# A fused token encoder, attention and routed LSTM kernel: cell work one unit later, fronts begun six units early, values' transfers from Sync, a feature-major projection

## The chip, the cores and the metric

The kernel runs on one core of one Trainium2 chip. The metric is the device time of one execution in microseconds (us): the median of three runs of the kernel before is 1920.38 us (1920.33 to 1920.73). The five engines are called PE (TensorE), DVE (VectorE), ACT (ScalarE), POOL (GpSimd) and SP (Sync, which here only issues transfers). Each runs its own list of instructions in order, and they meet at semaphores alone.

## What is computed

Sixteen sequences of 512 tokens go through three layers. The reference, cut to what matters:

```python
h = tok(x)                                    # embedding (89) next to an upsampled |STFT| projection (39)
h = h + attn(layernorm(h))                    # 8 heads of 16; 64 summary tokens and 448 feature tokens
h = h + ffn(layernorm(h))                     # top-2 of 8 LSTM experts

def attn(x):
    Q, K, V = split(x @ W_qkv + b_qkv)        # Q scaled
    out_wtok = softmax(Qw . Kcat) . Vcat      # each summary token over its own 7 feature tokens and itself
    w_wtok = softmax(Qf . out_wtok) per chunk # one weight of a feature token for its summary
    w_fea = softmax(Qf . K window of 17)      # local window
    out_fea = w_wtok * out_wtok + w_fea . V window
    return out @ W_out + b_out

def expert(x_seq, Wi, Wh, b, Wo, bo):         # scan over the 16 sequences, all 512 tokens side by side
    gates = xt @ Wi + h @ Wh + b
    c = sigmoid(f) * c + sigmoid(i) * tanh(g)
    h = sigmoid(o) * tanh(c)
    return h @ Wo + bo
# logits -> top 2 -> softmax of two; expert inputs are masked; y = sum of mask * weight * expert output
```

The scan is over the 16 sequences, so the LSTM state of 8 experts times 2 choices times 512 tokens passes from one sequence to the next.

## The kernel before

**Steps and units.** A step is one sequence. A step of the LSTM part has 32 units, `t = 0..31`, four for each expert `e = t // 4`: gates I, G, F, O in this order, `g = t % 4`. A unit on PE (`unit_gate`, L506) is twelve matmuls of 128x128 weights and 512 columns: input and state, each as three half-precision products for two choices. The timeline prints them as x6 from `xm` and x6 from `Hs`. Its result lies in one of two PSUM slots. ACT takes it out with a tanh (`gate_tanh`, L655), which frees the slot for the unit after next. DVE makes the cell and the hidden state: `input_part` (L1007), `cell` (L1013, L1017), `hidden` (L992), `hidden_lo` (L997), `chosen` (L1028, L1032, the tokens' choice times its weight), and `masked_input` (L985), which writes `xm`, the masked input of an expert that PE reads from the expert's unit I on. ACT adds `cell_tanh` (L662) and `split_hi` (L666, the upper half of the hidden state), on which `hidden_lo` waits. `unit_y` (L512) is the output matmul of an expert.

**Fronts.** Everything that a sequence needs before its LSTM step (embedding, layer norm, attention, second norm, logits, choice, masks) is its front: some 45 pieces, which `front(t, b)` of each engine issues in unit `t` of the step before. Which piece goes to which unit is set by the tables `SP_AT`, `PE_AT`, `ACT_AT` and `DVE_AT` (from L56). So every engine's list is written out by hand: step work and front pieces take turns, and each piece waits for the other engines by a semaphore of its own. Pieces of the front that are named below: `xn` (L795, layer norm's output), `p_lo` (L878) and `p_T` (L882, transposed window weights), `values` (L459, 84 small matmuls of window weights by values), `window` (L447, 84 of queries by keys), `proj` (L465, L466, attention's projection and its bias), `logits` (L477), `maskT` (L483), `emb` (L420). Queries and values go to a block-diagonal tile `diag` by four transfers each, from SP (queries, L284) and from ACT's own queue (values, L619), because the diagonal blocks lie on other partitions' columns.

**Masks.** At the end of a front the masks go to DRAM and come back spread over 128 partitions (`mask_in`, L338), and `masked_input` of the next step's expert 0 reads them in unit 30 (`XM_AT`).

The first front has no LSTM step to hide it and takes until 118.8 us; step 0 has no state term and no F gate; steps 1 to 14 are alike; step 15 has no front.

## Time and profile before

| | |
|---|---|
| median of three runs | 1920.38 us |
| the profiled execution | 1918.11 us, its span 1916.3 us |
| PE busy | 1729.1 us, 90% of the span |
| DVE busy | 1559.5 us, 81% |
| ACT busy | 991.9 us, 52% |
| POOL busy | 65.2 us, 3% |
| gate matmuls (L506) | 5904, 1451.6 us busy |
| chain that ended last | PE 40%, DVE 33%, DMA 8%, issue 7%, ACT 5%, ACT's queue 4% |
| mean granted clock of PE | 0.97 of full speed |

Busy time of an engine is a share of the span. The timeline prints instructions in order of time, merged where alike; the last bracket is the time that the engine sat idle before the row, and who ended it. A matmul's own duration has its way through the array in it, so the distance from one start to the next is what it costs PE.

### The profile page before, as it was taken

What the parts mean: (1) busy time and instruction counts of PE and PEld (TensorE: products, weight loads), DVE (VectorE), ACT (ScalarE), POOL (GpSimd) and SP (SyncE); (2) the same over time, 40 slices, a digit from 0 to 9 for tenths busy, and PEclk for the clock granted to TensorE, in tenths of its full rate; (3) what the DMA queues carried; (4) which work ended last, traced back from release to release, by engine and by line L of the source; (5) the groups of instructions that cost most, each with busy time, mean ns of one, the idle gap of its engine ahead of it and who ended that gap; (6) DMA issues with size and microseconds to landing.
All of it is one profiled execution on the core that took longest, in us unless ns stands there. A gap on an engine that the chain in (4) does not pass through costs nothing.

```text
span 1916.3 us, 25885 instructions
## 1 busy us (share of the span) xinstructions
PE 1729.1 (90%) x9898; PEld 837.6 (44%) x9898; DVE 1559.5 (81%) x2433; ACT 991.9 (52%) x1114; POOL 65.2 (3%) x42
## 2 busy tenths in 40 slices
PE   3457799999999999999999999999999999999998
PEld 2223344444444444444444444444444444444443
DVE  2649698897988889798898988889898888979865
ACT  3234554646555555645545455455555555564544
POOL 1000000000000000000000000000000000000000
PEclk9668899999999999999999999999999999999999
DMA  3113241413314132232313224151331413223221
GB/s 114 20 41 74 57 67 46 77 37 67 63 49 74 39 70 52 52 70 51 67 45 69 51 57 67 44 80 37 63 66 46 76 37 71 53 50 67 55 61 36
DMA packets 318594, 110.95 MB, mean 58 GB/s; under 512 B 240331, under 2 KB 299581, under 8 KB 318471
## 3 DMA queue, kind: packets, MB, share of 16 engines
q1 hardware_dynamic: 202758, 101.96, 23.9%
q10 hardware_dynamic: 115712, 7.34, 3.8%
q8 instruction: 78, 1.28, 0.3%
q14 instruction: 46, 0.37, 0.1%
HBM read 89.84 MB, written 4.74 MB: 49 GB/s over the span
## 4 chain that ended last, share of the span: by engine, by line
PE 40%; DVE 33%; DMA 8%; issue 7%; ACT 5%; ACTq 4%; SPq 1%; POOL 0%; DVEq 0%
PE gates L506 25%; ACTq L619 4%; DVE C L1017 4%; DVE tmp L1007 4%; DMA masks<-mask_scratch 3%; DVE tmp L1013 3%; DMA prod<-in_x_ids 3%; DVE xm L985 3%; PE yp L512 3%; DVE Hs L997 3%; DVE tmp L1028 3%; DVE xn L795 2%; PE FA L447 2%; ACT tmp L655 2%; PE FA L459 2%
## 5 line engine op out<-in xcount | busy, mean ns | idle before, releaser
L655 ACT ACTIVATE tmp<-gates,bias_sb 128x1024 f32<-128x1024 f32 x504 | 557.5, 1109 | 558.6 <-PE gates L506 496.1
L506 PE MATMUL gates<-xm,wi_sb 128*128 128x512 f16 x3024 | 747.3, 384 | 46.2 <-ACT tmp L655 31.0
L506 PE MATMUL gates<-Hs,wh_sb 128*128 128x512 f16 x2880 | 704.4, 381 | 0.0
L506 PEld LDWEIGHTS gates<-xm,wi_sb 128*128 128x128 f16 x3024 | 290.3, 99 | 435.3 <-issue 105.1
L506 PEld LDWEIGHTS gates<-Hs,wh_sb 128*128 128x128 f16 x2880 | 283.2, 98 | 344.3 <-issue 8.0
L662 ACT ACTIVATE tmp<-C 128x1024 f32<-128x1024 f32 x128 | 135.2, 1057 | 226.4 <-DVE C L1017 223.2
L992 DVE SCALAR_TENSOR_TENSOR tmp<-tmp 128x1024 f32<-128x1024 f32 x128 | 155.9, 1218 | 71.8 <-ACT tmp L662 71.8
L1007 DVE SCALAR_TENSOR_TENSOR tmp<-tmp 128x1024 f32<-128x1024 f32 x120 | 144.9, 1208 | 46.4 <-ACT tmp L655 44.9
L985 DVE TENSOR_TENSOR xm<-xs,masks 128x2048 f16<-128x2048 f16 x128 | 155.2, 1212 | 32.7 <-DMA masks<-mask_scratch 32.7
L997 DVE SCALAR_TENSOR_TENSOR Hs<-tmp,Hs 128x1024 f16<-128x1024 f32 x120 | 146.4, 1220 | 37.7 <-ACT Hs L666 36.7
L1013 DVE SCALAR_TENSOR_TENSOR tmp<-tmp,C 128x1024 f32<-128x1024 f32 x120 | 146.4, 1220 | 14.4 <-ACT tmp L655 14.0
L1017 DVE SCALAR_TENSOR_TENSOR C<-tmp 128x1024 f32<-128x1024 f32 x120 | 147.0, 1225 | 4.1
L666 ACT ACTIVATE Hs<-tmp 128x1024 f16<-128x1024 f32 x120 | 126.5, 1055 | 31.2 <-DVE tmp L992 30.7
L512 PE MATMUL yp<-z,wo_sb 128*128 128x512 f32 x256 | 134.9, 609 | 8.2 <-DVE z L1032 8.2
L1105 POOL TENSOR_TENSOR rstd<-veps,mhalf 128x4 f32<-128x4 f32 x32 | 61.6, 1926 | 1682.6 <-DVE veps L922 1114.8
L1032 DVE TENSOR_TENSOR z<-tmp,roww 128x512 f32<-128x512 f32 x128 | 88.6, 692 | 13.6 <-DVE tmp L1028 0.5
L1028 DVE COPY_PREDICATED tmp<-rowk,tmp 128x512 f32<-128x512 uint16 x128 | 93.0, 727 | 0.1
L512 PEld LDWEIGHTS yp<-z,wo_sb 128*128 128x128 f32 x256 | 48.0, 194 | 38.8 <-issue 12.2
L459 PE MATMUL FA<-vwin,diag 128*128 128x32 f16 x1344 | 36.3, 177 | 7.4 <-DVE vwin L882 7.4
L447 PEld LDWEIGHTS FA<-xn,diag 128*128 128x128 f16 x1344 | 38.2, 97 | 8.1 <-issue 5.5
L459 PEld LDWEIGHTS FA<-vwin,diag 128*128 128x128 f16 x1344 | 36.0, 96 | 12.5 <-DVE vwin L882 9.2
L447 PE MATMUL FA<-xn,diag 128*128 128x32 f16 x1344 | 39.1, 178 | 0.0
(155 smaller groups left out, 1218.9 us busy)
## 6 DMA issues: line engine op xcount, KB each, us to landing
masks<-mask_scratch SPq DMA_DIRECT2D x128, 256.0 KB, 5.0
roww<-mw_scratch SPq DMA_DIRECT2D x128, 256.0 KB, 4.0
rowk<-mask_scratch SPq DMA_DIRECT2D x128, 128.0 KB, 3.0
diag<-pr SPq DMA_DIRECT2D x64, 112.0 KB, 4.3
diag<-vwin ACTq DMA_DIRECT2D x64, 112.0 KB, 4.8
out_dram<-h SPq DMA_DIRECT2D x16, 256.0 KB, 3.7
C<-in_wi SPq DMA_DIRECT2D x1, 2048.0 KB, 10.9
C<-in_wh SPq DMA_DIRECT2D x1, 2048.0 KB, 15.6
```

The costliest lines, as they stand in the source:

```text
L506: last = mm(gates[:, slot, k * SEQ:(k + 1) * SEQ], w, v, start=(i < K), stop=(i >= len(seq) - K))
L512: mm(yp[:, :], wo_sb[:, e, :], z32[:, :], start=False, stop=(e == E - 1)).then_inc(s_y, 1)
L655: A(tmp[:, gate_at(gate, e), :], gates[:, (n - 1) % 2, :], ACT.Tanh, bias=bias_sb[:, e, gate:gate + 1], scale=UNSCALE).then_inc(s_tanh, 1)
L662: A(tmp[:, TANH_C, :], C[:, e, :], ACT.Tanh, scale=0.5).then_inc(s_tc, 1)
L666: A(Hs[:, e, HI, :], tmp[:, gate_at(O, e), :], ACT.Copy, scale=V_SCALE).then_inc(s_hhi, 1)
L985: TT(xm[:, e % 2, :, :, :], xv, mv_, ALU.mult).then_inc(s_xm, 1)
L992: STT(out=at, in0=at, scalar=1.0, in1=tmp[:, TANH_C, :], op0=ALU.add, op1=ALU.mult).then_inc(s_h, 1)
L997: STT(out=Hs[:, e, LO, :], in0=tmp[:, gate_at(O, e), :], scalar=V_SCALE, in1=Hs[:, e, HI, :], op0=ALU.mult, op1=ALU.subtract).then_inc(s_h ...
L1007: STT(out=at_i, in0=at_i, scalar=1.0, in1=at_g, op0=ALU.add, op1=ALU.mult).then_inc(s_u, 1)
L1013: STT(out=at_f, in0=at_f, scalar=1.0, in1=C[:, e, :], op0=ALU.add, op1=ALU.mult).then_inc(s_v, 1)
L1017: STT(out=C[:, e, :], in0=at_f, scalar=0.5, in1=tmp[:, gate_at(I, e), :], op0=ALU.mult, op1=ALU.add).then_inc(s_c, 1)
L1028: V.copy_predicated(at[:, 0:SEQ], rowk1[:, e % 2, :].bitcast(u16), at[:, SEQ:2 * SEQ]).then_inc(s_sel, 1)
```

## The change

It has these parts:

1. **Cell work a unit later.** `cell(e)` moves from unit 4e+2 to 4e+4, `cell_tanh` from 4e+3 to 4e+4, `hidden` from 4e+4 to 4e+5, `input_part` from 4e+1 to 4e+2, `split_hi` from 4e+4 to 4e+6, `hidden_lo` from 4e+5 to 4e+7, `chosen` from 4e+6 to 4e+7, `unit_y` from unit 4e+8 to 4e+9. The F gate (and tanh of the cell in it) has two buffers in place of one, and `z32` is gone.
2. **Fronts six units early.** `run_front` lets a front begin at unit -6, that is unit 26 of the step before; nearly all pieces move 2 to 4 units earlier.
3. **Values** are interleaved (upper and lower half next to each other, 4 bytes), transposed once as 4-byte words, and sent to `diag` by four transfers from SP in unit 7. `diag` is interleaved too, so the weights of `window` and `values` are read with a step of two elements.
4. **The projection** is one 128x512 matmul, feature-major, a copy with the bias on ACT, and four transposes back.
5. `masked_input` for the next step's expert 0 moves from the start of unit 30 to the end of unit 31; the weights' rows go out by a transfer and a semaphore of their own (`wout`).

```diff
-    SP_AT = dict(ids=0, qbd=6, rows=28)
-    PE_AT = dict(emb=1, xT=3, qkv=4, summary=7, window=8, feature=14, values=18, proj=21, x2T=23,
+    SP_AT = dict(ids=-6, qbd=3, vz=7, rows=27, wrow=30)
+    PE_AT = dict(emb=-3, xT=0, qkv=1, summary=4, window=6, feature=12, values=16, proj=18, projT=19, x2T=23,
                  logits=24, maskT=27)
-    DVE_AT = dict(onehot=0, moments=1, xn=2, pw=5, q_lo=5, kv_lo=6, v_win=7, w_max=8, s_max=9, s_sub=10, w_sum=11,
-                  w_out=12, s_sum=13, s_norm=14, f_max=15, p_lo=16, p_T=16, f_sum=17, f_part=18, attn=19,
-                  moments2=21, xn2=22, x_lo=24, choice1=25, choice2=25, weights=26)
-    MASKS_AT = 29
+    DVE_AT = dict(onehot=-4, moments=-2, xn=-1, pw=2, q_lo=2, kv_lo=3, v_win=4, w_max=5, s_max=7, s_sub=8, w_sum=9,
+                  w_out=10, s_sum=11, s_norm=12, f_max=13, p_lo=14, p_T=15, f_sum=16, f_part=16, attn=17,
+                  moments2=20, xn2=21, x_lo=24, choice1=24, choice2=25, weights=26)
+    EARLY = 6
+    MASKS_AT = 28
-    XM_AT = 30
+    XM_AT = 31
...
+        def run_front(front, t, s):
+            if s == 0 and t == 0:
+                for u in range(-EARLY, 0):
+                    front(u, 1)
+            if s + 1 < STEPS:
+                front(t, s + 1)
+            if s + 2 < STEPS and t >= NG * E - EARLY:
+                front(t - NG * E, s + 2)
...
+                if t == SP_AT["vz"]:
+                    sp.wait_ge(S["vwin"], b + 1)
+                    sp.wait_ge(S["S"], b + 1)
+                    for g in range(NG):
+                        load(diag[32 * g:32 * g + 32, :, g, :], vwj[32 * g:32 * g + 32, :, :], S["vz"])
...
                 if t == PE_AT["proj"]:
                     pe.wait_ge(S["attn"], b1)
+                    mm(FA[:, 1, :], wout_sb[:, :], attn[:, :], start=True, stop=True).then_inc(S["projT"], 1)
+                if t == PE_AT["projT"]:
+                    pe.wait_ge(S["projS"], b1)
                     for i in range(TILES):
-                        mm(FB[:, i * D:(i + 1) * D], attn[:, i * P:(i + 1) * P], wout_sb[:, :], start=True, stop=False)
-                        last = mm(FB[:, i * D:(i + 1) * D], ones1[:, :], bout_sb[:, :], start=False, stop=True)
+                        last = nc.tensor.transpose(FB[:, i * D:(i + 1) * D], xnT[:, i * P:(i + 1) * P], ident[:, :])
...
-                    for v in (HI, LO):
-                        own = vhl[:, v, :]
-                        win = bass.AP(tensor=own.tensor, offset=own.offset, ap=[list(own.ap[0]), [QB, NBLK], [1, KB]])
-                        last = V.transpose(vw16[:, v, :, :], win)
-                    last.then_inc(S["vwin"], 1)
+                    win = bass.AP(tensor=vp.tensor, offset=vp.offset, ap=[list(vp.ap[0]), [QB, NBLK], [1, KB]])
+                    V.transpose(vwj, win).then_inc(S["vwin"], 1)
...
+                    if g == 0 and e and not first:
+                        cell(s, e - 1)
+                    elif g == 0 and s >= 2 and not e:
+                        cell(s - 1, E - 1)
                     if g == 1 and e < E - 1:
                         masked_input(s, e + 1, par, first and e == 0)
-                    if g == 1 and e and not last:
+                    if g == 3 and e and not last:
                         hidden_lo(s, e - 1)
...
-                    if t == XM_AT and not last:
-                        masked_input(s + 1, 0, 1 - par, False)
-                    if g == 2 and e:
+                    if g == 3 and e:
                         chosen(s, e - 1)
...
+                    run_front(lambda u, b: front(u, b, b % 2), t, s)
+                    if g == 1 and e:
+                        hidden(s, e - 1)
...
+                    if g == 2:
                         input_part(s, e, first)
-                    if g == 2 and not first:
-                        cell(s, e)
+                    if t == XM_AT and not last:
+                        masked_input(s + 1, 0, 1 - par, False)
```

**How the rows move: the end of a step on DVE.** These are DVE's rows of the kernel before from `hidden_lo` of expert 6 (written `Hs`) to the first `cell` (`C`) of the last expert; the `xm` row is the masked input on which unit 0 of the next step waits. The bracket is what a row waits for.

```order
L997 SCALAR_TENSOR_TENSOR Hs<-tmp,Hs 128x1024 [waits s_hhi]
L1007 SCALAR_TENSOR_TENSOR tmp<-tmp 128x1024 [waits s_tanh]
L985 TENSOR_TENSOR xm<-xs,masks 128x2048 [waits s_gate,f_xlo,s_mask_in0]
L1028 COPY_PREDICATED tmp<-rowk,tmp 128x512 [waits s_hlo,s_row_in0]
L1032 TENSOR_TENSOR z<-tmp,roww 128x512 [waits s_sel,s_y]
L1013 SCALAR_TENSOR_TENSOR tmp<-tmp,C 128x1024 [waits s_tanh]
L1017 SCALAR_TENSOR_TENSOR C<-tmp 128x1024 [waits s_u,s_v]
```

And these are the same rows of the changed kernel, from `input_part` of expert 7 (L1028 there) on:

```order
L1028 SCALAR_TENSOR_TENSOR tmp<-tmp 128x1024 [waits s_tanh]
L1018 SCALAR_TENSOR_TENSOR Hs<-tmp,Hs 128x1024 [waits s_hhi]
L1049 COPY_PREDICATED tmp<-rowk,tmp 128x512 [waits s_hlo,s_row_in0]
L1051 TENSOR_TENSOR tmp<-tmp,roww 128x512 [waits s_sel]
L819 TENSOR_SCALAR xn<-h_sb,mv,rstd 128x128 [waits f_rstd]
L819 TENSOR_SCALAR xn<-h_sb,mv,rstd 128x128 x3
L1006 TENSOR_TENSOR xm<-xs,masks 128x2048 [waits s_gate,f_xlo,s_mask_in0]
```

What moved: `xm` stood behind `hidden_lo` by one row of unit 29 and ahead of `chosen`; now it stands behind `hidden_lo`, `chosen` and the four rows of the next front's `xn`, and `hidden_lo` itself stands in unit 31.

**The same place on ACT**, in the changed kernel: the tanh rows (L678) are those of units 28, 29, 30 and 31, and L689 is `split_hi` of expert 6, which releases the `Hs` row above (`s_hhi`).

```order
L678 ACTIVATE tmp<-gates,bias_sb 128x1024 [waits s_c,s_gate]
L685 ACTIVATE tmp<-C 128x1024 [waits s_c]
L678 ACTIVATE tmp<-gates,bias_sb 128x1024 [waits s_c,s_gate]
L605 ACTIVATE h_sb<-FB 128x512 [waits f_h2,f_emb]
L678 ACTIVATE tmp<-gates,bias_sb 128x1024 [waits s_h,s_gate]
L689 ACTIVATE Hs<-tmp 128x1024 [waits s_h]
L678 ACTIVATE tmp<-gates,bias_sb 128x1024 [waits s_y,s_gate]
```

What moved: `split_hi` came in unit 28 behind one tanh; it now comes behind the tanh of unit 30.

**The window weights on DVE.** Before, `p_T` (L882) follows `p_lo` (L878) at once, in unit 16, and PE's `values` wait for it after unit 18:

```order
L992 SCALAR_TENSOR_TENSOR tmp<-tmp 128x1024 [waits s_tanh,s_tc]
L878 SCALAR_TENSOR_TENSOR pr<-vwin,pr 128x896 [waits f_phi]
L882 STREAM_TRANSPOSE vwin<-pr 128x896 [waits f_plo]
L985 TENSOR_TENSOR xm<-xs,masks 128x2048 [waits s_gate,s_mask_in1]
L997 SCALAR_TENSOR_TENSOR Hs<-tmp,Hs 128x1024 [waits s_hhi]
```

Now, in units 13 to 15, with PE's `values` after unit 16:

```order
L1013 SCALAR_TENSOR_TENSOR tmp<-tmp 128x1024 [waits s_tanh,s_tc]
L899 SCALAR_TENSOR_TENSOR pr<-vwin,pr 128x896 [waits f_phi]
L1028 SCALAR_TENSOR_TENSOR tmp<-tmp 128x1024 [waits s_tanh]
L1018 SCALAR_TENSOR_TENSOR Hs<-tmp,Hs 128x1024 [waits s_hhi]
L1049 COPY_PREDICATED tmp<-rowk,tmp 128x512 [waits s_hlo,s_row_in0]
L1051 TENSOR_TENSOR tmp<-tmp,roww 128x512 [waits s_sel]
L903 STREAM_TRANSPOSE vwin<-pr 128x896 [waits f_plo]
```

What moved: `p_T` stands behind `input_part`, `hidden_lo` and `chosen`, in the unit right ahead of the one after which PE wants it, instead of two units ahead.

## Rows read from the trace of the kernel before

**Rows 1.** Busy time and PE's timeline, one step from its unit 18 to the next
```profile
core 0: us, PE busy (x) PEld busy (x) DVE busy (x) ACT busy (x) POOL busy (x), PEclk, DMA share, GB/s
624.55:738.61 114.06, 108.16 (x631) 52.45 (x631) 98.08 (x153) 61.72 (x70) 3.82 (x2) 1.00 0.28 58
...
624.55 1.47 PE L506 MATMUL gates<-xm,wi_sb 128*128 128x512 f16 x6 [1.46 <-ACT tmp L655]
...
661.03 0.63 PE L483 MATMUL FB<-ident,pr 128*72 128x128 f32 x4 [1.15 <-DVE pr L973]
```

**Rows 2.** Timeline of ACT behind its four transfers of values
```profile
717.80 2.12 ACT L655 ACTIVATE tmp<-gates,bias_sb 128x1024 f32<-128x1024 f32 x2 [3.09 <-issue]
```

**Rows 3.** Timeline of PE: projection, one output matmul, logits
```profile
637.88 0.38 PE L465 MATMUL FB<-wout_sb,attn 128*128 128x128 f32 x2
...
641.10 1.47 PE L506 MATMUL gates<-xm,wi_sb 128*128 128x512 f16 x6
...
650.15 1.02 PE L512 MATMUL yp<-z,wo_sb 128*128 128x512 f32 x2
651.04 1.06 PE L477 MATMUL FA<-rw_sb,xnT 128*128 128x8 f32 x8
651.95 1.46 PE L506 MATMUL gates<-xm,wi_sb 128*128 128x512 f16 x6
```

**Rows 4.** Timeline of all engines around the end of a step
```profile
666.58 1.05 ACT L666 ACTIVATE Hs<-tmp 128x1024 f16<-128x1024 f32 x1
667.53 1.46 PE L506 MATMUL gates<-xm,wi_sb 128*128 128x512 f16 x6
667.66 1.23 DVE L997 SCALAR_TENSOR_TENSOR Hs<-tmp,Hs 128x1024 f16<-128x1024 f32 x1 [1.94 <-ACT Hs L666]
667.74 1.11 ACT L655 ACTIVATE tmp<-gates,bias_sb 128x1024 f32<-128x1024 f32 x1
...
671.49 1.23 DVE L985 TENSOR_TENSOR xm<-xs,masks 128x2048 f16<-128x2048 f16 x1 [1.38 <-DMA masks<-mask_scratch]
...
672.82 1.46 PE L506 MATMUL gates<-xm,wi_sb 128*128 128x512 f16 x6
```

**Rows 5.** Timeline of DVE: durations of pieces, and a stretch without idle time
```profile
624.86 1.11 DVE L882 STREAM_TRANSPOSE vwin<-pr 128x896 f32<-128x896 f32 x1
...
630.32 0.72 DVE L1028 COPY_PREDICATED tmp<-rowk,tmp 128x512 f32<-128x512 uint16 x1
...
631.76 0.22 DVE L892 TENSOR_TENSOR red<-oW,red 128x64 f32<-128x64 f32 x1
...
645.90 1.11 DVE L795 TENSOR_SCALAR xn<-h,mv,rstd 128x128 f32<-128x128 f32 x4
...
725.80 1.22 DVE L985 TENSOR_TENSOR xm<-xs,masks 128x2048 f16<-128x2048 f16 x1
...
737.68 1.18 DVE L878 SCALAR_TENSOR_TENSOR pr<-vwin,pr 128x896 f16<-128x896 f32 x1
```

**Rows 6.** Timeline of PE: the 84 matmuls of `values`
```profile
627.15 2.25 PE L459 MATMUL FA<-vwin,diag 128*128 128x32 f16 x84
629.25 1.46 PE L506 MATMUL gates<-xm,wi_sb 128*128 128x512 f16 x6
```

**Rows 7.** PE's timeline in step 0, and two short stretches with the clock (columns as in rows 1)
```profile
207.19 1.07 PE L483 MATMUL FB<-ident,pr 128*72 128x128 f32 x4 [5.46 <-DVE pr L973]
...
216.71 1.83 PE L506 MATMUL gates<-xm,wi_sb 128*128 128x512 f16 x6 [2.37 <-issue]
...
207.20:210.70 3.50, 3.50 (x11) 1.89 (x12) 1.07 (x1) 1.17 (x2) 0.00 (x0) 0.50 0.61 120
217.50:220.90 3.40, 3.40 (x11) 1.35 (x9) 1.69 (x2) 0.00 (x0) 0.00 (x0) 0.52 0.20 58
```

**Rows 8.** Transfers by issue: count, size, us from issue to landing
```profile
diag<-pr SPq DMA_DIRECT2D x64, 112.0 KB, 4.3
diag<-vwin ACTq DMA_DIRECT2D x64, 112.0 KB, 4.8
```

More of the change, by code:

```diff
@@ L361, in step @@
                     e, g = t // NG, t % NG
-                    if t == 9 and not first:
+                    if t == 10 and not first:
                         store(s - 1, 1 - par)
-                    if not last:
-                        front(t, s + 1)
+                    run_front(front, t, s)
                     if g == 1 and e < E - 2:
@@ L373, in step @@
                         rows_in(s + 1, 0)
-            for t in range(NG * E):
+            for t in range(-EARLY, NG * E):
                 front(t, 0)
@@ L532, in step @@
                         unit_gate(s, e, g, first)
-                    if g == 0 and e == 2:
+                    if g == 1 and e == 2:
                         y_bias(s)
-                    if g == 0 and e >= 2:
+                    if g == 1 and e >= 2:
                         unit_y(s, e - 2)
-                    elif g == 0 and not first:
+                    elif g == 1 and not first:
                         unit_y(s - 1, e - 2 + E)
@@ L540, in step @@
                         y_back(s - 1)
-                    if not last:
-                        front(t, s + 1)
+                    run_front(front, t, s)
             pe.wait_ge(s_const, 16 * len(consts))
             pe.wait_ge(s_zero, 1)
-            pe.wait_ge(s_prep, 4)
-            for t in range(NG * E):
+            pe.wait_ge(s_prep, 3)
+            for t in range(-EARLY, NG * E):
                 front(t, 0)
@@ L659, in cell_tanh @@
                 act.wait_ge(s_c, s * E + e + 1)
-                if s == 0 and e:
-                    act.wait_ge(s_h, e)
-                A(tmp[:, TANH_C, :], C[:, e, :], ACT.Tanh, scale=0.5).then_inc(s_tc, 1)
+                if s == 0 and e >= 2:
+                    act.wait_ge(s_h, e - 1)
+                A(tmp[:, gate_at(F, e), :], C[:, e, :], ACT.Tanh, scale=0.5).then_inc(s_tc, 1)
             def split_hi(s, e):
@@ L678, in step @@
                         y_out(s - 1)
-                    if g == 0 and e and not last:
+                    if g == 0 and e:
+                        cell_tanh(s, e - 1)
+                    elif g == 0 and not first:
+                        cell_tanh(s - 1, E - 1)
+                    if g == 2 and e and not last:
                         split_hi(s, e - 1)
-                    elif g == 0 and not e and not first:
+                    elif g == 2 and not e and not first:
                         split_hi(s - 1, E - 1)
-                    if g == 3:
-                        cell_tanh(s, e)
-                    if not last:
-                        front(t, s + 1)
+                    run_front(front, t, s)
             par_of = lambda b: PAR[0]
@@ L706, in _ @@
             split_w_hi(wh_st, wh_sb, 0.5, s_wh_load)
-            for t in range(NG * E):
+            for t in range(-EARLY, NG * E):
                 front(t, 0)
@@ L714, in _ @@
             run_steps(step_p)
+            cell_tanh(STEPS - 1, E - 1)
             y_out(STEPS - 1)
@@ L1061, in step @@
                         add_y(s - 1, 1 - par)
-                    if not last:
-                        front(t, s + 1, 1 - par)
-                    if g == 1:
+                    run_front(lambda u, b: front(u, b, b % 2), t, s)
+                    if g == 1 and e:
+                        hidden(s, e - 1)
+                    elif g == 1 and not first:
+                        hidden(s - 1, E - 1)
+                    if g == 2:
                         input_part(s, e, first)
-                    if g == 2 and not first:
-                        cell(s, e)
+                    if t == XM_AT and not last:
+                        masked_input(s + 1, 0, 1 - par, False)
             dve.wait_ge(s_zero, 1)
-            for t in range(NG * E):
+            for t in range(-EARLY, NG * E):
                 front(t, 0, 0)
@@ L1081, in _ @@
             run_steps(step)
+            cell(STEPS - 1, E - 1)
             hidden(STEPS - 1, E - 1)
@@ L1107, in step @@
             def step(s, par, first, last):
-                if not last:
-                    for t in range(NG * E):
-                        front(t, s + 1)
+                for t in range(NG * E):
+                    run_front(front, t, s)
             pool.wait_ge(s_zero, 1)
-            for t in range(NG * E):
+            for t in range(-EARLY, NG * E):
                 front(t, 0)
```

108 lines of the change are left out of this document (53 added, 55 removed).

## The prediction

> **What bounds the kernel now.** The page comes first: PE is busy for 90% of the span, DVE for 81%, and steps 1 to 14 look alike, so I read one step closely. From unit 18 of one step to unit 18 of the next there are 114.06 us, of which PE is busy for 108.16, DVE for 98.1 and ACT for 61.7 [rows 1]. The reader is to see three things. PE does the most, and idles for 5.9 us a step. That idle time is a few waits of about 1 us for ACT or DVE, two of which are shown [rows 1]. And DVE, with 86% of the step, has little room where the front is dense. The average step is 114.0 us: unit 0 of step 1 starts at 216.71 [rows 7], unit 0 of step 5 at 672.82 [rows 4], a fourth of the difference. The sum therefore is: PE's own work per step, plus the waits that remain or appear, against 114.0, times 14.
>
> The timelines of ACT and DVE then tell where waits come from. The longest idle time on ACT that is nobody's work is 3.09 us behind its own four transfers of values [rows 2]: a tanh is late, DVE waits for it, and PE for the next one.
>
> **PE's own work.** The projection costs PE 641.10 - 637.88 = 3.22 us [rows 3]. The new one is one 128x512 matmul in full precision, like the output matmul, 651.04 - 650.15 = 0.89 us, and four transposes, 0.63 at most as `maskT` shows [rows 1]: 1.5 us. That takes off 1.7 and leaves 108.2 - 1.7 = 106.5 us per step. The new copy on ACT (0.6 to 0.7) lies beside unit 19. The strided weights of `window` and `values` I cost at nothing, see below.
>
> **The waits that go.** ACT no longer issues the values' transfers, which takes the 3.1 us out of unit 9 and 10. SP does it in unit 7; behind it on SP stand rows for `chosen` eight units later, so its wait for the window scores delays nobody. DVE transposes once instead of twice, 1.1 us less. `emb`, `xT` and `x2T` get one more unit between DVE's piece and PE's, and the token ids are fetched in unit 26 for a piece in unit 28. If I walk PE and DVE through the step with durations of the trace, all 5.9 us of old waits go: what I find late in their place is next.
>
> **A new wait at the end of a step.** PE's unit 0 reads `xm`. In the kernel before, `xm` came in unit 30, waited for the masks' transfer, and was just in time: it ended at 672.72 and PE began at 672.82 [rows 4]. Now it is the last of a chain that can't start before PE ends unit 30. Tanh starts 0.21 after the unit's matmuls are through (a tanh at 667.74 behind a unit that ended at 667.53) and lasts 1.11; `split_hi` to `hidden_lo` is 667.66 - 666.58 = 1.08; `hidden_lo` lasts 1.23 [rows 4]; `chosen` takes 631.76 - 630.32 = 1.44, the four pieces of `xn` 1.11 [rows 5]; `xm` 1.23 and 0.10 to PE [rows 4]. The sum is 7.5 us. In the meantime PE has only unit 31, which is half of 672.72 - 667.53, 2.6 us. So PE waits 4.9 us, in every step, whatever DVE did before. Moving `xm` to unit 31 costs nothing only where DVE runs ahead of PE, and here the chain forbids it.
>
> **A new wait before `values`.** DVE's `hidden_lo` of unit 11 can't start before unit 10 ends plus 0.21 + 1.11 + 1.08 = 2.4 us. From there to `p_lo` DVE has the same nine pieces as in the stretch from 725.80 to 737.68, which had no idle time: `xm`, `hidden_lo`, `s_sum`, `input_part`, `chosen`, `s_norm`, `cell`, `f_max`, `hidden`, 11.9 us; `p_lo` adds 1.18 [rows 5]. Then follow `hidden_lo` 1.23, `chosen` 1.44 and `p_T` 1.11: 2.4 + 11.9 + 1.2 + 3.8 = 19.3 us after unit 10. PE arrives there after six units (15.6), one output matmul (0.9) and the matmul of the feature scores (0.8): 17.3. It waits 2.0 us. Before, `p_T` stood two units ahead of `values` and this wait did not exist.
>
> With both, a step has 106.5 + 4.9 + 2.0 = 113.4 us, 0.6 less than now. The work saved is about given back.
>
> **The clock.** What decides is what such gaps do to PE's clock. In step 0, PE idles 5.46 us before 207.19, and in the next 3.5 us its granted clock is 0.50, the lower level of 1.2 GHz; it idles 2.37 before 216.71, and the next 3.4 us are at 0.52 [rows 7]. In the step of rows 1, with waits of 1.5 at most, it stays at 1.00. At half speed and fully busy, 3.4 us lose 1.7. After 4.9 us of idle time I count that loss in every step. After 2.0 us, which is less than the 2.37 shown and more than the 1.5 shown, I take half of it, 0.9. So a step has 113.4 + 1.7 + 0.9 = 116.0 us, 2.0 more than now, and 14 steps have 28 us more. The bounds are no loss (113.4) and both in full (116.8).
>
> **What runs once.** In the first front the chain goes through both sets of transfers, 4.3 and 4.8 us to landing [rows 8], with pieces twice as long now; through the projection, at the slow clock; and through one transpose fewer: between 0 and some 8 us less. In step 0 six units of the next front stand in unit 0, where PE must wait for each, up to 6 us more; the last boundary lacks `xn`, 1 us less. I take -4 together, between -9 and +5.
>
> **Strided weights.** The 84 matmuls of `values` take 2.10 us, 25 ns each with their weights, which lie packed [rows 6]. No row shows weights with a step of two. The nearest row for slow weight loads are the eight full-precision ones of `logits`, 0.91 us, 114 ns each [rows 3]. So the price lies between 0 and 84 x 89 ns = 7.5 us for each of two groups per step. I take 0, since the moving operand of `values` has that step already. The Trainium skill's page "TensorE: Matmul & The Clock Gate", section "Weight-path perf modes — Fast Weight Load (FWL) and DoubleRow", says that half-precision weights load fast, packed or strided, for column steps up to 1,024 elements; by it the price is 0. No run here shows it yet, and by the other end the sum would be 240 us higher.
>
> **Sum.** 1918.11 (this execution) + 28 - 4 = 1942; the median of the runs is 2.3 above this execution, so 1944 us.
>
> **The rivals.**
> - *The clock holds.* The gaps are there but each falls so that the clock stays up, or falls only while PE idles. For it: in steps 1 to 14 the clock is near 1 although there are waits. Against: both gaps of rows 7. Then 14 x -0.6 - 4 = -12: 1908 us. This is the case on the other side. It decides at a loss of 0.6 us per step: with less, the kernel is faster.
> - *The waits are hidden* because DVE's and ACT's new slack is larger than I read it, and PE runs without waits. 14 x (106.5 - 114.0) - 4 = -109: 1811 us. Against it: the order of ACT and DVE makes both chains hard.
> - *Strided weights load slowly.* Two groups per step; with a third of the bound, 2.5 us each, 16 x 5 = 80 more: about 2020, at the bound 2180.
> - *The parts cancel*, for instance if the clock falls at the boundary alone and the loss overlaps the gap by half (0.85): 14 x 0.2 - 4, about 1919.
>
> **Chances.** A measurement of this kernel can tell some 0.2% from no change, 4 us. The forecast (both waits and the clock) gets 0.62, the strided weights 0.08: slower 0.70. The clock holding gets 0.14 and the hidden waits 0.06: faster 0.20. Cancelling gets 0.10, and is the chance of no difference. The range goes from just under the clock holding, 1907, to both losses in full and the upper bound of what runs once, 1920.4 + 14 x 2.8 + 5 = 1965, taken as 1966; it leaves out the hidden waits, the slow weights and a small tail, under 0.2.
>
> **What would show it.** PE idles for about 4.9 us before unit 0 of each step, and the waits put it down to `xm`; it idles for about 2 before the first matmul of `values`, put down to `p_T`; the granted clock reads 0.5 for a stretch behind unit 0 of nearly all steps, and the mean is below 0.97. The waits behind ACT's issue are gone, and the projection costs 1.5 us. If a step is 113.4 with the clock at 1.00, the clock was wrong; if PE does not wait at unit 0, the chain was; if `values` takes more than 2.1 us between its neighbours, the weights were.

## The result: 0.3% slower, and where the expected 1% went

The changed kernel takes 1926.62 us (median of 8 runs, 1923.51 to 1927.87) against 1920.36 for the kernel before (8 runs, 1917.91 to 1922.06) in the same session: ratio 1.0032, 95% interval 1.0021 to 1.0043. That is 6.3 us slower where 24 were forecast. The time lies in the range; the change was forecast almost four times too large.

| | before | after |
|---|---|---|
| span of the profiled execution | 1916.3 us | 1924.2 us |
| PE busy | 1729.1 us | 1720.4 us |
| DVE busy | 1559.5 us | 1548.0 us |
| mean granted clock | 0.97 | 0.946 |
| start of unit 0 in step 1 (us from the span's start) | 216.71 | 208.97 |
| start of unit 0 in step 15 | 1812.41 | 1817.50 |

The last two rows split the result. Ahead of step 1 the change is 7.7 us faster. The 14 steps from there to step 15 take 1608.53 us against 1595.70, which is 12.8 more, or 114.90 against 113.98 each. The rest, step 15 and the tail, takes 2.8 more. So +7.9 between the two spans. The 14 steps of the changed kernel are not quite alike: steps 2 to 13 take 115.16 on average (1381.93 / 12, below) where the kernel before has 113.92, and step 14 only 112.0, since no front begins in it.

**The new wait at the end of a step.** The same stretch as in [rows 4], all engines, in the changed kernel's timeline:

```profile
662.25 1.11 ACT L678 ACTIVATE tmp<-gates,bias_sb 128x1024 f32<-128x1024 f32 x1 [2.10 <-PE gates L533]
...
663.26 1.05 ACT L689 ACTIVATE Hs<-tmp 128x1024 f16<-128x1024 f32 x1
663.35 1.46 PE L533 MATMUL gates<-Hs,wh_sb 128*128 128x512 f16 x6
664.34 1.22 DVE L1018 SCALAR_TENSOR_TENSOR Hs<-tmp,Hs 128x1024 f16<-128x1024 f32 x1 [1.54 <-ACT Hs L689]
...
665.67 0.73 DVE L1049 COPY_PREDICATED tmp<-rowk,tmp 128x512 f32<-128x512 uint16 x1
666.43 0.69 DVE L1051 TENSOR_TENSOR tmp<-tmp,roww 128x512 f32<-128x512 f32 x1
667.04 1.11 DVE L819 TENSOR_SCALAR xn<-h_sb,mv,rstd 128x128 f32<-128x128 f32 x4
...
668.06 1.22 DVE L1006 TENSOR_TENSOR xm<-xs,masks 128x2048 f16<-128x2048 f16 x1
```

This is the chain of the prediction, row by row: the tanh of unit 30, `split_hi`, `hidden_lo`, `chosen`, `xn`, `xm`. PE is through with unit 31 at 664.81 (663.35 + 1.46) and starts unit 0 at 669.38. The changed kernel's timeline of PE, for that unit and for the stretch around the projection:

```profile
624.23 1.02 PE L489 MATMUL FA<-attn,wout_sb 128*128 128x512 f32 x2
625.09 1.46 PE L533 MATMUL gates<-xm,wi_sb 128*128 128x512 f16 x6
...
627.68 0.60 PE L493 MATMUL FB<-ident,xnT 128*128 128x128 f32 x4
628.11 1.24 PE L533 MATMUL gates<-xm,wi_sb 128*128 128x512 f16 x5
...
669.38 2.48 PE L533 MATMUL gates<-xm,wi_sb 128*128 128x512 f16 x6 [4.58 <-issue]
671.66 2.16 PE L533 MATMUL gates<-Hs,wh_sb 128*128 128x512 f16 x6
673.66 0.60 PE L452 MATMUL FB<-ident,xn 128*128 128x128 f32 x4
...
729.41 2.30 PE L484 MATMUL FA<-vwin,diag 128*128 128x32 f16 x84 [1.92 <-DVE vwin L903]
731.56 2.72 PE L533 MATMUL gates<-xm,wi_sb 128*128 128x512 f16 x6
734.07 1.68 PE L533 MATMUL gates<-Hs,wh_sb 128*128 128x512 f16 x6
735.59 1.02 PE L539 MATMUL yp<-tmp,wo_sb 128*128 128x512 f32 x2
```

PE waits 4.58 us at unit 0 (the profile calls the releaser "issue", although `xm` is what ends just before, at 669.28) and 1.92 before `values`. Both gaps are there in every one of steps 2 to 14. The units behind them are slow: unit 0 takes 673.66 - 669.38 = 4.28 us and the unit behind `values` 735.59 - 731.56 = 4.03, where a unit at full clock takes 2.59. The projection costs 0.86 + 0.43 = 1.29 us, where [rows 3] show 3.22. `values` costs 731.56 - 729.41 = 2.15 against 2.10 in [rows 6]; experiment 2, where the clock does not fall there, shows 2.11.

The same over steps 2 to 13 and over the one step shown, from unit 0 to unit 0 (columns as in [rows 1]), and two stretches behind the gaps:

```profile
323.58:1705.51 1381.93, 1303.75 (x7441) 628.45 (x7442) 1168.18 (x1813) 754.85 (x840) 45.98 (x24) 0.96 0.27 57
669.38:784.20 114.82, 108.31 (x621) 52.29 (x621) 97.34 (x152) 62.98 (x70) 3.83 (x2) 0.96 0.25 57
669.40:672.80 3.40, 3.40 (x9) 1.24 (x10) 3.37 (x3) 0.00 (x0) 0.00 (x0) 0.54 0.60 149
731.60:734.00 2.40, 2.40 (x11) 0.82 (x8) 2.26 (x7) 1.06 (x1) 0.00 (x0) 0.50 0.51 83
```

Idle time of PE in the one step is 114.82 - 108.31 = 6.51 us, and 4.58 + 1.92 = 6.50: of the old waits none is left. The granted clock behind both gaps is 0.50 to 0.54, the level of 1.2 GHz. There is one boundary more than the 14 steps have. The last one, before step 15, has no `xn` in its chain and a gap of 3.56, and unit 0 behind it is slow too:

```profile
1817.50 2.72 PE L533 MATMUL gates<-xm,wi_sb 128*128 128x512 f16 x6 [3.56 <-issue]
```

These are the lines of the transfers, in the form of [rows 8]:

```profile
diag<-pr SPq DMA_DIRECT2D x64, 112.0 KB, 3.1
diag<-vwin SPq DMA_DIRECT2D x64, 112.0 KB, 3.3
```

### The profile page after: what moved, and what is told of

Same layout as the page of the kernel before. It is cut to its first block, busy times and chain, and to the rows that moved or that the text cites. A ratio compares the mean times of both kernels' runs of the same rounds, so it can differ in the third digit from the quotient of the medians.

```text
span 1924.2 us, 25452 instructions
## 1 busy us (share of the span) xinstructions
PE 1720.4 (89%) x9738; PEld 828.2 (43%) x9738; DVE 1548.0 (80%) x2416; ACT 1009.0 (52%) x1130; POOL 64.4 (3%) x42
## 4 chain that ended last, share of the span: by engine, by line
PE 80%; DVE 11%; issue 4%; ACT 2%; DMA 1%; SPq 1%; POOL 0%; DVEq 0%; ACTq 0%
PE gates L533 62%; PE yp L539 5%; PE FA L484 2%; PE FA L472 2%; PE FA L457 1%; DVE tmp L1013 1%; DVE Hs L1018 1%; DVE xm L1006 1%; ACT tmp L678 1%; PE FB L445 1%; DVE pr L899 1%; DVE vwin L903 1%; DVE vwin L896 1%; PE yp L546 1%; DVE tmp L1028 1%
## 5 line engine op out<-in xcount | busy, mean ns | idle before, releaser
L678 ACT ACTIVATE tmp<-gates,bias_sb 128x1024 f32<-128x1024 f32 x504 | 559.6, 1111 | 646.6 <-PE gates L533 646.5
L533 PE MATMUL gates<-xm,wi_sb 128*128 128x512 f16 x3024 | 770.3, 393 | 80.9 <-issue 70.0
L533 PE MATMUL gates<-Hs,wh_sb 128*128 128x512 f16 x2880 | 720.0, 387 | 0.0
L533 PEld LDWEIGHTS gates<-xm,wi_sb 128*128 128x128 f16 x3024 | 298.0, 100 | 486.3 <-issue 208.6
L533 PEld LDWEIGHTS gates<-Hs,wh_sb 128*128 128x128 f16 x2880 | 287.9, 100 | 359.1 <-issue 33.7
L1028 DVE SCALAR_TENSOR_TENSOR tmp<-tmp 128x1024 f32<-128x1024 f32 x120 | 146.3, 1219 | 3.3 <-ACT tmp L678 3.3
L539 PE MATMUL yp<-tmp,wo_sb 128*128 128x512 f32 x256 | 134.5, 607 | 6.3 <-DVE tmp L1051 6.3
L689 ACT ACTIVATE Hs<-tmp 128x1024 f16<-128x1024 f32 x120 | 126.0, 1050 | 14.4 <-DVE tmp L1013 13.1
L1051 DVE TENSOR_TENSOR tmp<-tmp,roww 128x512 f32<-128x512 f32 x128 | 88.6, 692 | 4.4
L825 DVE TENSOR_TENSOR prod<-qT,kw 128x64 f32<-128x64 f32 x16 | 4.4, 275 | 75.1 <-ACT kf L624 75.1
L539 PEld LDWEIGHTS yp<-tmp,wo_sb 128*128 128x128 f32 x256 | 47.6, 192 | 36.2 <-issue 12.4
## 6 DMA issues: line engine op xcount, KB each, us to landing
diag<-pr SPq DMA_DIRECT2D x64, 112.0 KB, 3.1
diag<-vwin SPq DMA_DIRECT2D x64, 112.0 KB, 3.3
```

The source lines that it names most:

```text
L533: last = mm(gates[:, slot, k * SEQ:(k + 1) * SEQ], w, v, start=(i < K), stop=(i >= len(seq) - K))
L539: mm(yp[:, :], wo_sb[:, e, :], chosen_at(e), start=False, stop=(e == E - 1)).then_inc(s_y, 1)
L678: A(tmp[:, gate_at(gate, e), :], gates[:, (n - 1) % 2, :], ACT.Tanh, bias=bias_sb[:, e, gate:gate + 1], scale=UNSCALE).then_inc(s_tanh, 1)
L689: A(Hs[:, e, HI, :], tmp[:, gate_at(O, e), :], ACT.Copy, scale=V_SCALE).then_inc(s_hhi, 1)
L1028: STT(out=at_i, in0=at_i, scalar=1.0, in1=at_g, op0=ALU.add, op1=ALU.mult).then_inc(s_u, 1)
```

## The experiments

Ratios are to the kernel before, run on the same chip in the same session. In experiments 1 to 4 "my theory" is that of the prediction: PE's own work, plus the two new waits, plus the clock. "Slow time" below is the total of stretches at half the clock within steps 1 to 14; it is 116.9 us in the changed kernel and 17.1 in the kernel before.

**1. `xm` a unit earlier** (at the end of unit 30; before the change it stood at the start of that unit)

```diff
-    XM_AT = 31
+    XM_AT = 30
```

> The changed kernel with the masked input of the next step's expert 0 at the end of unit 30 instead of 31, ahead of hidden_lo, chosen and xn. A step of the changed kernel is 114.9 us: I read it as 105.2 of PE's own work, two waits of 4.58 and 1.93 (each with 0.17 of a matmul's tail), and 2.85 lost to the slow clock behind them. My theory (the chain to xm holds PE, and its gap costs a slow stretch): the wait at unit 0 goes, with 1.8 us of slow clock; xn is then the last of the chain and makes PE wait 1.0 us before xT, after unit 0. So 114.9 - 4.75 - 1.8 + 1.1 = 109.5 us a step, about 1848 us. Rival 1, the masks' transfer: xm is asked for 7 us earlier and waits for the masks instead, and PE still waits 2 us or more at unit 0, 1880 us or more. Rival 2, DVE is the bound over the step and the wait reappears at another place in full: 1915 to 1927 us.

Measured 1839.41 us (1837.79 to 1840.96), ratio 0.9582 (0.9568 to 0.9597). The wait at unit 0 is gone from step 2 on, and steps 2 to 13 take 109.3 us. In its place `xn` makes PE wait 0.82 before `xT`, as expected. The masks' transfer, rival 1, does not hold PE. The other gap stays, and with it the slow clock, here in every step, by PE's timeline of this kernel:

```profile
594.32 2.34 PE L484 MATMUL FA<-vwin,diag 128*128 128x32 f16 x84 [1.93 <-DVE vwin L903]
596.50 2.63 PE L533 MATMUL gates<-xm,wi_sb 128*128 128x512 f16 x6
```

One number in a table, and a change that loses 0.3% gains 4%. The wait and its clock cost 87 us together, 9 more than expected.

**2. `p_T` a unit earlier**

```diff
-                  w_out=10, s_sum=11, s_norm=12, f_max=13, p_lo=14, p_T=15, f_sum=16, f_part=16, attn=17,
+                  w_out=10, s_sum=11, s_norm=12, f_max=13, p_lo=14, p_T=14, f_sum=16, f_part=16, attn=17,
```

> The changed kernel with p_T right behind p_lo in unit 14, ahead of input_part, hidden_lo and chosen, as the kernel before had it. My theory: PE's 1.93 us before values go with 0.17 of tail and about 1.2 us of slow clock per step, 3.3 x 14 = 46 us less: about 1880 us, with the wait at unit 0 unchanged at 4.6. Rival (hidden_lo is now later by 1.1 us and delays something else, or the chain at the step's end takes up the time): less than 15 us gained.

Measured 1893.06 us (1892.37 to 1894.64), ratio 0.9865 (0.9848 to 0.9881). The gap before `values` is gone, and with it the slow clock there:

```profile
717.72 2.25 PE L484 MATMUL FA<-vwin,diag 128*128 128x32 f16 x84
719.83 1.46 PE L533 MATMUL gates<-xm,wi_sb 128*128 128x512 f16 x6
```

13 us of the expected gain are not there: the projection now waits 1.3 us for `attn`, since PE arrives earlier and DVE does not.

**3. Both**

The two edits together.

> Both of the two edits. My theory: they add, 77 + 46 us, so about 1803 us, with a step of 106.2 us, the clock at 1.00 in steps 1 to 14, and PE's only wait there about 1 us before xT. Rival: DVE, with 97.3 us of work a step, can't follow and waits of over 3 us a step appear elsewhere: 1830 us or more.

Measured 1818.12 us (1816.03 to 1819.4), ratio 0.947 (0.9456 to 0.9485). No stretch of steps 2 to 14 is slow any more. The window of steps 2 to 13, and what is left before the projection:

```profile
316.41:1607.16 1290.75, 1265.13 (x7441) 616.18 (x7440) 1169.69 (x1813) 754.31 (x840) 45.99 (x24) 1.00 0.29 61
```

```profile
598.59 1.12 PE L489 MATMUL FA<-attn,wout_sb 128*128 128x512 f32 x2 [1.33 <-DVE attn L924]
```

Here PE is busy for 1265.13 / 12 = 105.43 us in a step of 107.56, with all parts of the change in place. The prediction had put PE's work at 106.5. The two edits together give 108 us where the theory had 123; it lacked the wait of 1.33 before the projection. One by one they gave 87 and 34, together 12 more than at once, since each alone also takes part of the other's slow clock: PE's busy time in steps 2 to 13 is 108.65 us in the changed kernel, 106.5 in experiment 1, 106.7 in experiment 2 and 105.4 here.

**4. The clock alone: the wait filled with work.** Behind unit 31, PE runs 20 matmuls of 448 columns whose result is overwritten.

```diff
+                if t == -1 and not is_zero(b):
+                    pe.wait_ge(S["hsb"], b1)
+                    for _ in range(FILL):
+                        mm(FB[:, 0:HB * KB], identb[:, :],
+                           bandb[:, :].rearrange("p (a k) -> p a k", a=1).to_broadcast([P, HB, KB]),
+                           start=True, stop=True)
```

> The changed kernel, with 20 extra matmuls of 448 columns on PE behind unit 31 (they write a PSUM bank that the transposes xT overwrite, so nothing uses them; 0.19 us each, 3.8 us), which fill most of the 4.58 us in which PE waits for xm. The chain to xm is untouched, so without an effect of the clock the time stays within 2 us of 1926.6 (the theory that the clock costs nothing, and that something else makes a step 114.9). My theory: the slow stretch behind unit 0 goes and only that: 1.6 to 1.9 us per step, 22 to 27 us less, 1900 to 1905 us, with unit 0 taking 2.6 us instead of 4.3 to 5.0.

Measured 1893.7 us (1892.24 to 1894.81), ratio 0.9865 (0.985 to 0.9879). `xm` comes no earlier, but unit 0 starts at full clock:

```profile
658.93 3.95 PE L452 MATMUL FB<-bandb,identb 128*128 128x448 bf16 x20
663.69 1.46 PE L540 MATMUL gates<-xm,wi_sb 128*128 128x512 f16 x6 [0.81 <-issue]
...
666.28 0.60 PE L459 MATMUL FB<-ident,xn 128*128 128x128 f32 x4
```

Unit 0 takes 2.59 us again. The way from PE's last group of unit 31 to unit 0 is 663.69 - 657.64 = 6.05 us, against 669.38 - 663.35 = 6.03 in the changed kernel, so the wait for `xm` is as long as it was. The 14 steps take 112.71 on average, 2.2 us less, the kernel 33 us less; the expectation had 22 to 27. So the clock's part at this boundary is shown apart from the wait's: about 2.2 of the boundary's cost in each step. The changed kernel's own trace agrees: its unit 0 takes 4.2 to 5.1 us, 2.2 more than 2.59 on average.

**5. Values' transfers from SP, in the kernel before**, in unit 9, where ACT issued them.

```diff
-    SP_AT = dict(ids=0, qbd=6, rows=28)
+    SP_AT = dict(ids=0, qbd=6, vz=9, rows=28)
...
-                if t == ACT_AT["vz"]:
-                    act.wait_ge(S["vwin"], b1)
-                    act.wait_ge(S["S"], b1)
-                    for g in range(NG):
-                        act.dma_start(diag[32 * g:32 * g + 32, :, :, g, :].rearrange("p v j d -> p (v j) d"),
...
+                if t == SP_AT["vz"]:
+                    sp.wait_ge(S["vwin"], b + 1)
+                    sp.wait_ge(S["S"], b + 1)
+                    for g in range(NG):
+                        load(diag[32 * g:32 * g + 32, :, :, g, :].rearrange("p v j d -> p (v j) d"),
...
```

> The kernel before with one part of the change alone: the four transfers of the values issued by SP in unit 9 instead of by ACT (64-byte pieces and the two transposes stay). My theory: ACT's 3.1 us behind its own issue are what makes PE wait before units 12 and 18 (0.7 and 1.46 us, each with 0.17 of tail), so these go: 2.5 x 14 = 35 us less, about 1885 us. Rival: from unit 5 to 16 DVE's own work is longer than PE's, so DVE only idles less and PE waits as before at unit 18: 1912 us or more.

Measured 1901.66 us (1899.99 to 1902.28), ratio 0.9926 (0.9911 to 0.9941), between the two. PE waited 29 times for ACT's tanh, two times in a step and about 1.07 us each; now it is once, 14 times 1.23:

```profile
PE gates L512 <- ACT tmp L654: 17.2, 14, 1.2
```

The wait that went, 0.5 to 0.9 us before unit 12, stood behind ACT's issue ([rows 2]). The one that stayed is that of [rows 1], before unit 18. It is 0.2 shorter, so the issue was not its main cause, and moving the transfers alone is worth 14 us, between theory (35) and rival (8 or less).

**6. The best version.** Experiment 3, with DVE's front pieces of units 17 and 31 (`attn`, `xn`) ahead of the step's own work in those units.

```diff
+    FRONT_FIRST = (17, 31)
...
+                    if t in FRONT_FIRST:
+                        run_front(lambda u, b: front(u, b, b % 2), t, s)
...
-                    run_front(lambda u, b: front(u, b, b % 2), t, s)
+                    if t not in FRONT_FIRST:
+                        run_front(lambda u, b: front(u, b, b % 2), t, s)
```

> The kernel of e3 with DVE's front piece ahead of the step work in two units: in unit 17 (attn ahead of the masked input) and in unit 31 (xn ahead of hidden_lo and chosen). e3's steps are 107.56 us: 105.2 of PE's own work, 1.33 of waiting before the projection, 0.7 to 0.9 before xT, and tails. My theory: both waits go, 2.1 us per step, so 1818 - 30 = 1788 us, steps of 105.4 us. Rival (hidden_lo or the masked input of expert 5, now up to 1.5 us later, make another wait, since DVE is 92% busy): 1805 us or more.

Measured 1800.69 us (1800.27 to 1801.38), ratio 0.9401 (0.9387 to 0.9415): 6% under the kernel before and 6.3% under the change as it stands. One step of its windows:

```profile
638.75:745.28 106.53, 105.57 (x621) 51.41 (x621) 97.48 (x152) 62.65 (x71) 3.83 (x2) 1.00 0.26 62
```

PE is busy for 99% of it. The largest wait left is 0.4 to 0.6 us, before `qkv`; three small ones make 0.9 us a step. The theory had 1788 us; 14 times 0.9 is the 13 us that it lacked. From here little but less work on PE can make a step shorter.

**7. The old projection, in that version**

```diff
-                    mm(FA[:, 1, :], wout_sb[:, :], attn[:, :], start=True, stop=True).then_inc(S["projT"], 1)
-                if t == PE_AT["projT"]:
-                    pe.wait_ge(S["projS"], b1)
...
-                        last = nc.tensor.transpose(FB[:, i * D:(i + 1) * D], xnT[:, i * P:(i + 1) * P], ident[:, :])
+                        mm(FB[:, i * D:(i + 1) * D], attn[:, i * P:(i + 1) * P], wout_sb[:, :], start=True, stop=False)
+                        last = mm(FB[:, i * D:(i + 1) * D], ones1[:, :], bout1[:, :], start=False, stop=True)
```

> The kernel of e6 with the projection of the kernel before (eight small matmuls in pairs, bias by a row of ones) in unit 18. My theory: 3.22 us of PE's time instead of 0.86 and 0.43, so 1.93 x 16 = 31 us more than e6, and now and then a slow stretch of the clock behind it, as the kernel before has in 4 of its steps (1.7 us each, up to 7 in all): 1819 to 1826 us if e6 is 1788. Rival (the slow stretches come nearly every step, since nothing else delays PE): 1840 us or more.

Measured 1843.27 us (1840.22 to 1846.13), ratio 0.9622 (0.9608 to 0.9637): 42.6 us more than experiment 6. Steps 2 to 13 take 109.38 us instead of 106.46. Of the 2.92, 1.9 are the work. The clock costs 1.5: PE is busy for 108.8 us on average, and for 107.28 in a step without a slow stretch. PE's waits are shorter by the rest. The clock falls behind the old projection although PE hardly waits there:

```profile
710.08 0.49 PE L493 MATMUL FB<-wout_sb,attn 128*128 128x128 f32 x2 [0.19 <-DVE attn L923]
...
713.00 0.48 PE L494 MATMUL FB<-bout,ones 1*128 1x128 f32 x2
713.41 2.74 PE L534 MATMUL gates<-xm,wi_sb 128*128 128x512 f16 x6
715.95 1.89 PE L534 MATMUL gates<-Hs,wh_sb 128*128 128x512 f16 x6
```

The unit behind it takes 717.68 - 713.41 = 4.27 us (the next row starts at 717.68). This happens in 9 of steps 2 to 14 of this kernel, not in all: in the step before, the unit at 605.53 is at full speed.

**8. Cell work in its old units, in that version**: `cell`, `cell_tanh`, `hidden`, `split_hi`, `hidden_lo`, `chosen`, `input_part` back where the kernel before has them, the rest as in experiment 6.

```diff
-                    if g == 0 and e:
-                        cell_tanh(s, e - 1)
...
+                    if g == 3:
+                        cell_tanh(s, e)
...
-                    if g == 1 and e:
-                        hidden(s, e - 1)
...
+                    if g == 0 and e:
+                        hidden(s, e - 1)
...
-                    if g == 2:
+                    if g == 1:
...
+                    if g == 2 and not first:
+                        cell(s, e)
```

> The kernel of e6 with the cell work, hidden and chosen back in the units of the kernel before (the F gate keeps two buffers, output matmuls stay a unit later). My theory: the cell of an expert is then due one unit, 2.6 us, earlier, and the slack that I worked out for the changed order is 1.3 us behind the densest units, so PE waits for ACT's tanh by 1 to 1.5 us at one to three places of a step: 20 to 50 us more than e6, 1808 to 1838. Rival (moving the cell is worth nothing, the early fronts and the free ACT queue are what helps): within 5 us of e6.

Measured 1889.9 us (1886.71 to 1894.9), ratio 0.987 (0.985 to 0.9891): 89 us more than experiment 6, far above the upper bound. Two waits of PE appear in every step, 2.3 us at unit 0 and 3.0 before the logits. The timeline around the second shows its mechanism:

```profile
631.33 1.23 DVE L1036 SCALAR_TENSOR_TENSOR C<-tmp 128x1024 f32<-128x1024 f32 x1
632.59 1.06 ACT L686 ACTIVATE tmp<-C 128x1024 f32<-128x1024 f32 x1 [3.31 <-DVE C L1036]
633.55 0.58 ACT L653 ACTIVATE xnT<-FB 128x512 f32<-128x512 f32 x1
...
634.18 1.06 PE L505 MATMUL FA<-rw_sb,xnT 128*128 128x8 f32 x8 [3.03 <-ACT xnT L653]
```

ACT stands at `cell_tanh` for 3.31 us until DVE has the cell; the copy that PE wants waits behind it. In experiment 6 ACT waits for the cell too (up to 3.3 us), but no `cell_tanh` stands right ahead of that copy.

The first wait has another cause:

```profile
656.87 1.22 DVE L1036 SCALAR_TENSOR_TENSOR C<-tmp 128x1024 f32<-128x1024 f32 x1
658.01 1.22 DVE L1004 TENSOR_TENSOR xm<-xs,masks 128x2048 f16<-128x2048 f16 x1
```

`xm` is still at the end of unit 30, and the two pieces of `cell` (2.4 us) now stand ahead of it there; in the kernel before they stood behind it. So the 89 us are the price of the old cell units together with this place of `xm`; how they divide was not tried.

**9. Fronts in their old units, in that version** (new projection in units 20 and 21)

```diff
-    EARLY = 6
-    FRONT_FIRST = (17, 31)
-    MASKS_AT = 28
+    EARLY = 0
+    FRONT_FIRST = (19,)
+    MASKS_AT = 29
...
-    PE_AT = dict(emb=-3, xT=0, qkv=1, summary=4, window=6, feature=12, values=16, proj=18, projT=19, x2T=23,
+    PE_AT = dict(emb=1, xT=3, qkv=4, summary=7, window=8, feature=14, values=18, proj=20, projT=21, x2T=23,
```

> The reordered kernel of the experiment before (1800.7 us), with the fronts back in the units that they had before the change (EARLY = 0, tables of before; the projection stays new, one unit apart, in units 20 and 21). Cell work, values' transfers and projection stay as changed. Theory one (the early fronts' worth is the waits of a unit's front piece for DVE): the waits before emb (1.0 us), xT (1.6), x2T (1.2) and maskT (1.4) that the kernel before shows come back, at most 5.2 us in each of 14 steps; together some 50 us: 1850, between 1825 and 1875. Rival (with the cell a unit later DVE runs far enough ahead that these waits stay away): no more than 15 us, under 1816.

Measured 1942.31 us (1937.32 to 1949.62), ratio 1.0142 (1.0114 to 1.017): 141 us more than experiment 6 (by the medians), and slower than any other kernel here. Both theories fall. Of the waits that the theory wanted back only a part comes (up to 2.1 us before `emb` in 8 of 14 steps, 0.3 before `x2T` and `maskT`), and the large ones are others. The kernel before waits at most 0.5 us at unit 0 in steps 2 to 14; here the end of a step reads:

```profile
669.30 1.11 ACT L679 ACTIVATE tmp<-gates,bias_sb 128x1024 f32<-128x1024 f32 x1 [0.53 <-PE gates L534]
670.95 1.23 DVE L1007 TENSOR_TENSOR xm<-xs,masks 128x2048 f16<-128x2048 f16 x1 [3.88 <-DMA masks<-mask_scratch]
...
672.27 1.02 PE L534 MATMUL gates<-xm,wi_sb 128*128 128x512 f16 x4 [3.01 <-issue]
```

The masks leave a unit later than in the change, and DVE stands 3.88 us at `xm` in wait for their transfer, with PE behind it, 2.4 to 3.6 us in steps 2 to 14. `values` waits 1.8 us again (`p_T` in unit 16 has the later cell work ahead of it here; that this is the reason was not tried), and the transposes of the projection wait 0.7 to 2.0 for ACT's copy. The clock falls behind the first two in most steps: slow time 86.3 us. So, with these tables, a later cell without earlier fronts is worse than neither. How the 141 us divide between the masks' unit and the rest was not tried.

**10. The new projection alone, in the kernel before** (units 20 and 21)

```diff
-    PE_AT = dict(emb=1, xT=3, qkv=4, summary=7, window=8, feature=14, values=18, proj=21, x2T=23,
+    PE_AT = dict(emb=1, xT=3, qkv=4, summary=7, window=8, feature=14, values=18, proj=20, projT=21, x2T=23,
...
-    ACT_AT = dict(h=1, xT=3, qkv=4, split=5, summary=9, window=11, vz=9, pr_hi=15, feature=16, x2T=23,
+    ACT_AT = dict(h=1, xT=3, qkv=4, split=5, summary=9, window=11, vz=9, pr_hi=15, feature=16, proj=20, x2T=23,
```

> The kernel before with the new projection alone (one 128x512 matmul, a copy with the bias on ACT, four transposes; in units 20 and 21, where the old one stood in 21). Theory one (the projection's gain goes to the end of a step in full): 1.93 us less for PE in each of 16 fronts, and the four slow-clock stretches of 3.4 us behind the old projection gone (1.7 us each): 1920 - 27 - 7 = 1886. Rival (in the kernel before DVE sets the pace of a step together with PE, so what PE saves it then waits for): 1910 or more.

Measured 1914.19 us (1913.06 to 1915.51, 10 runs) against 1915.36, ratio 0.9992 (0.9982 to 1.0001): nothing. The rival holds. The window of a step, and PE's new wait:

```profile
785.77:899.85 114.08, 106.52 (x620) 50.81 (x621) 98.10 (x153) 62.00 (x70) 3.82 (x2) 1.00 0.29 58
```

```profile
636.11 1.13 PE L463 MATMUL FA<-attn,wout_sb 128*128 128x512 f32 x2 [1.42 <-DVE attn L906]
```

A step is as long as before (113.7 on average, against 114.0). PE has 1.9 us less work and waits for `attn` before the projection, 1.4 us, where [rows 3] have no wait, and there is no slow stretch left. The kernel before waits for DVE's and ACT's pieces at six or seven places in a step, and what PE saves between two of them it waits at the next.

## Why the prediction was right in its sign and wrong in its size

- **The new wait at the end of a step**, 4.9 from start to start: measured 4.58 of idle time and 0.17 of the matmul before it (see below), 4.75. Right, with its chain. Experiment 1 takes it away by one number.
- **The new wait before `values`**, 2.0: measured 1.92 and 0.17, 2.1. Right, and experiment 2 takes it away.
- **All old waits go**: right, 6.51 us of idle time are the two new waits.
- **Strided weights at nothing**: right, 2.15 against 2.10 us for 84 matmuls. The rule of the Trainium skill's page "TensorE: Matmul & The Clock Gate", section "Weight-path perf modes — Fast Weight Load (FWL) and DoubleRow", that strided half-precision weights load fast, agrees with this row for a step of two. Where the clock stays up (experiment 2) the 84 take 719.83 - 717.72 = 2.11.
- **The clock**, 2.6 us in a step: measured 3.2 (PE's busy time in steps 2 to 13, 1303.75 / 12 = 108.65, less the 105.43 of experiment 3, where two waits are left as well and the clock is full). So it was too small by 0.6. Of the 3.2 some 2.2 belong to the end of a step by experiment 4. Unit 0 was slow at all 15 boundaries, and at 12 of them the clock was low for 6.8 us, part of it still idle time, where the prediction counted 3.4; the unit behind `values` was slow in 10 of the 14 steps, where the prediction took half of the loss. That the second came out near one half is luck: nothing in rows 7 said so.
- **What runs once**, -4 between -9 and +5: measured -9.5, if the 14 steps are counted at 115.16 - 113.92 = 1.24 each (7.9 - 17.4). It is -7.7 ahead of step 1; step 1 is no longer than before, and step 14 some 3 us shorter than its neighbours; and +2.8 behind step 15's start, which is the 15th slow unit 0. The forecast had no clock there. Too large by 5.5, at the edge of its range.
- **PE's own work: this is the step that failed.** The prediction took PE's busy time, 108.16, less 1.7 for the projection: 106.5. Both terms were mis-sized, the first by more. A group of six matmuls is listed with 1.46 us, but the next group starts 1.29 us after it: the last 0.17 of a group, its tail, lies under the next one. Where PE then idles, nothing lies over the tail. It stands in the busy time, and the idle time is counted from its end. The step of [rows 1] has six idle times, so 1.0 of the 108.16 was counted as work and added again with the waits, and PE's own work was near 107.1. The projection saves 3.22 - 1.29 = 1.93, not 1.7. That makes 105.2. Experiment 10 bears it out with only the projection changed: 106.52 busy, less the tails of eight idle times, is 105.2. Experiment 3 is busy for 105.43 with two idle times, experiment 6 for 105.57 with three: both leave 105.1 without the tails.

Put right, the sum reads 105.1 + 4.58 + 1.93 + 0.34 (two tails) = 111.95, and with the clock's 3.2, 115.15: what steps 2 to 13 take (115.16). The clock's term comes from the same busy time, so this shows that the parts fit, not each of them apart; experiment 4 shows the larger share of the clock by itself. The error of 1.4 us in the work is about 1% of a step, but it stands in a difference: the prediction compared 116.0 with 114.0, the truth was 115.2 against 113.9. Over 14 steps the work was put 20 us too high and the clock 8 too low, and what runs once 5.5 too high. Together that is about the distance of forecast and result, 1944 against 1926.6. Without the clock's error on the other side the miss would have been larger.

The rivals: the clock did not hold (experiment 4). The waits were not hidden in the change as it stands; taken away (experiments 3 and 6) they give 1818 and 1801, on both sides of the prediction's 1811 for that case. That is near by luck in part, since the 106.5 that it took for a step without waits is 105.1 of work, and in experiment 6 the rest is short waits with their tails. Cancelling (about 1919) lies nearer to the result than the forecast, but not for its reason: the loss did not overlap the gap, the work came out 1.4 us lower.

What a part is worth depends on the others. Taken out of the best version, the projection costs 43 us, the cell's place 89 (with `xm` behind it), the early fronts 141, together more than twice the 115 us that this version gains on the kernel before. Put alone into the kernel before, the projection gives nothing and SP's issue 14.

## What to carry to other kernels

When a change makes waits vanish and others appear, compare work with work: take what an engine does from start to next start, leave the tails ahead of idle times out, and only then add waits, since an error of 1% in the work outweighs the effect looked for. Where a piece is moved by a unit in a list written by hand, follow each chain that crosses the new place to its end; here a gain of 5.3% hung on two numbers in a table. And a saving on an engine that waits at several places shows only once these waits are gone, so judge it in the version without them.
